# Two chained self-attention layers: stage 1's q and k masked and stacked by VectorE from PSUM, with new engine orders

## The chip, the core and the metric

The kernel runs on one core of a Trainium2 chip. The metric is the device time of one execution in microseconds (us). Engine names in rows are those of the profile: PE is TensorE's matmul, PEld its weight load, DVE VectorE, ACT ScalarE, POOL GpSimd, SP SyncE (which only issues DMAs here).

## The reference

Two self-attention layers run one after the other on x of shape (4, 128, 32, 32), that is 4 batches of 128 channels and 1024 positions. Each layer computes, for every batch:

```
q = Wq x + bq          # 16 x 1024
k = Wk x + bk          # 16 x 1024
v = Wv x + bv          # 128 x 1024
attn = softmax(q^T k)  # 1024 x 1024, over the last axis
x = gamma * (v attn^T) + x
```

All data is fp32. The second layer takes the first layer's x.

## The kernel before

**Stages.** The work is cut into eight stages s, one for each layer and batch: stages 0 to 3 are layer 0, stages 4 to 7 layer 1. Stage s + 4 needs the x that stage s finished. Inside a stage the 1024 positions are eight tiles of 128.

**What one stage does.** TensorE projects q and k together into one PSUM tile (steps `QX` and `QK`, two accumulating halves). The result is stored as fp32r, three copies of a 16-row block for each of q and k, and one of the copies is replaced by the rounding rest: a *mask* step makes a rounded copy of the masked rows, and a *stack* step subtracts that from the whole. The stacked tile `qk` is copied by two DMAs with its halves swapped (`qk_swapped`, step `swap`), and the energies are products of the two. For each tile i, TensorE makes energies (`E.s.i`), VectorE takes the negated row maximum (`max.s.i`, L563), and ScalarE takes the exponential in place and its row sum (`sum.s.i`, L472). The logarithm of the sums (`log`), split in two by GpSimd (`parts`), transposed by TensorE (`shift`), copied to SBUF by VectorE (`rows`) and placed by DMA into spare rows of `qk` (`place`), turns a second, transposed energy product (`ET.s.k`) into the logarithm of the softmax, so that one exponential (`attn`, L484) gives the finished weights. Six of eight weight tiles are cut into a high and a low part (`hi` L359, L490; `lo` L364, L558) and multiplied with a cut v (`PH`, `PV`); the other two are multiplied whole. v is projected by `VX` and `V` and evacuated by VectorE (`v32`). VectorE adds the result to x (`finish`).

**The ring.** All products but those of the weights with v go into a ring of three PSUM tiles, `ring0` to `ring2`. A step named `E.0.3.0` uses ring tile 0. Before TensorE writes a ring tile, it waits for whoever reads the tile's previous content last (`wait_for_ring`): for an energy tile that is the `sum` step, for q and k it is the evacuation.

**Stage 0 and stage 1.** Stage 0's energies are computed from plain fp32 q and k (`qk_raw`, `swapped_raw`) so that they can start early. Stage 1 is listed in `FROM_SBUF`: ScalarE copies its q and k from PSUM to the SBUF tile `unstacked` (`evac.1.0`, L466), GpSimd masks (`mask.1.0`, L407) and stacks (`stack.1.0`, L414) from there. Stages 2 to 7 have mask and stack on VectorE, both read from PSUM (L530, L537).

**Orders.** Each engine works through a list written by hand, in order: `PE_ORDER`, `ACT_ORDER`, `DVE_ORDER`, `POOL_ORDER`, `SP_ORDER`. An instruction that waits holds up everything behind it on its engine. `warm.0.n` on TensorE are n pairs of products of zeros, which write to `out_psum` and depend on nothing. `swap.1.0` stands first and `swap.0.0` second on SP's list. These lines decide who waits in the part that the diff touches:

```python
elif what == "E":
    engine.wait_ge(sum_made, nth_sum[s, i])
elif what == "QK":
    engine.wait_ge(*(evacuated, nth_evac[s, 0]) if s in FROM_SBUF else stacked(s))
```

Of the kernel before, what the change touches and what calls it, by code (L numbers as in the profile page):

```python
# [48 lines left out]


PE_ORDER = """
raw.0.0.0 raw.0.1.1 E.0.6.2 QX.1.0.0 E.0.0.1 QK.1.0.0 E.0.7.2 warm.0.2 E.0.4.0 E.0.2.1 E.0.1.2 warm.0.2 E.0.3.0
E.0.5.1 VX.0.0.2 warm.0.2 E.1.4.0 V.0.0.2 shift.0.0.1 warm.0.2 E.1.7.1 warm.0.2 QX.2.0.0 E.1.6.2 QK.2.0.0 warm.0.2
ET.0.2.1 warm.0.4 ET.0.3.2 warm.0.2 E.1.5.1 ET.0.1.0 E.1.0.2 PH.0.2 E.1.2.0 PH.0.3 shift.0.1.1 E.1.3.2 ET.0.0.1
E.1.1.0 PH.0.1 E.2.4.1 PV.0.0 E.2.7.2 ET.0.6.0 PV.0.3 VX.1.0.1 E.2.1.0 V.1.0.1 shift.1.1.2 PV.0.1 ET.0.4.2 PV.0.2
ET.0.5.0 QX.3.0.1 ET.0.7.2 E.2.3.0 QK.3.0.1 E.2.0.2 PV.0.7 ET.1.3.0 PH.0.5 ET.1.2.2 PH.0.6 E.2.6.0 ET.1.1.1 PV.0.5
E.2.2.2 PH.0.4 E.2.5.1 PV.0.6 PV.0.4 VX.2.0.0 ET.1.4.2 V.2.0.0 ET.1.6.1 PH.1.3 ET.1.5.2 PH.1.1 ET.1.7.0 ET.1.0.1
E.3.0.2 PH.1.2 shift.2.1.0 PV.1.2 E.3.1.1 QX.4.0.0 E.3.2.2 QK.4.0.0 PV.1.0 ET.2.3.1 PV.1.3 PV.1.1 ET.2.1.2 ET.2.2.0
E.3.6.1 E.3.5.2 PH.1.6 E.3.4.0 PH.1.5 PV.1.6 E.3.3.1 PH.1.4 E.3.7.2 PV.1.7 E.4.4.0 ET.2.6.1 PV.1.5 PV.1.4 VX.3.0.2
ET.2.4.1 V.3.0.2 ET.2.5.0 PH.2.3 ET.2.0.1 PH.2.1 ET.2.7.2 PV.2.3 shift.3.1.0 E.4.0.1 PH.2.2 E.4.7.0 E.4.1.2 PV.2.0  # L60
E.4.2.1 PV.2.2 PV.2.1 QX.5.0.0 ET.3.3.2 QK.5.0.0 ET.3.0.1 PH.2.6 ET.3.1.2 PH.2.4 ET.3.2.1 PV.2.6 ET.3.4.2 E.4.5.0
PH.2.5 E.4.6.1 PV.2.4 PV.2.5 ET.3.6.2 PV.2.7 ET.3.5.0 VX.4.0.2 E.4.3.1 V.4.0.2 E.5.3.0 PV.3.0 E.5.4.1 PH.3.2 E.5.6.2
shift.4.1.0 PH.3.3 E.5.2.0 PH.3.1 E.5.1.1 PV.3.3 PV.3.1 PV.3.2 QX.6.0.2 ET.4.3.0 QK.6.0.2 ET.4.2.1 PH.3.4 ET.3.7.0
E.5.7.1 PH.3.6 ET.4.1.0 PV.3.6 E.5.5.2 PH.3.5 E.5.0.0 PV.3.5 PV.3.7 E.6.6.1 ET.4.5.2 PV.3.4 VX.5.0.0 ET.4.4.2
V.5.0.0 ET.4.0.1 PH.4.3 ET.4.6.2 PV.4.3 E.6.3.0 QX.7.0.1 shift.5.1.2 PV.4.0 ET.4.7.2 E.6.2.0 QK.7.0.1 PH.4.1 PH.4.2
ET.5.1.2 PV.4.1 PV.4.2 ET.5.2.0 ET.5.3.1 ET.5.6.2 E.6.4.0 PH.4.4 E.6.0.2 PH.4.6 E.6.7.1 PH.4.5 E.6.5.0 PV.4.6 PV.4.5
E.6.1.2 PV.4.4 PV.4.7 ET.5.0.1 E.7.0.0 ET.5.5.2 E.7.4.1 PH.5.1 E.7.1.2 PV.5.0 shift.6.1.0 PH.5.3 E.7.6.1 ET.5.4.0
PV.5.1 E.7.3.2 PH.5.2 PV.5.3 PV.5.2 VX.6.0.0 E.7.2.1 ET.6.0.2 V.6.0.0 PH.5.5 ET.5.7.2 PH.5.4 ET.6.5.0 PH.5.6
ET.6.2.1 E.7.7.2 PV.5.5 PV.5.7 ET.6.4.0 ET.6.1.1 PV.5.6 PV.5.4 VX.7.0.2 E.7.5.0 ET.6.6.1 V.7.0.2 PH.6.1 PV.6.0
ET.6.7.1 ET.6.3.2 shift.7.1.0 PH.6.6 PH.6.4 PH.6.5 PH.6.3 PH.6.2 ET.7.3.0 ET.7.2.2 PV.6.2 PV.6.1 PV.6.3 PV.6.6  # L70
PV.6.5 PV.6.4 ET.7.0.1 ET.7.1.0 ET.7.6.2 PV.6.7 PH.7.2 ET.7.5.1 ET.7.4.0 ET.7.7.2 PV.7.2 PH.7.3 PV.7.0 PH.7.1 PH.7.6
PV.7.1 PV.7.3 PH.7.5 PH.7.4 PV.7.6 PV.7.5 PV.7.4 PV.7.7
"""
ACT_ORDER = """
sum.0.6 evac.1.0 sum.0.0 sum.0.7 sum.0.4 sum.0.2 sum.0.1 sum.0.3 log.0.0 sum.0.5 sum.1.4 v_hi.0.0 log.0.1 sum.1.7
sum.1.6 attn.0.2 attn.0.3 attn.0.1 sum.1.5 sum.1.0 sum.1.2 attn.0.0 sum.1.3 sum.1.1 sum.2.4 attn.0.6 log.1.1 sum.2.7
sum.2.1 attn.0.4 attn.0.5 attn.0.7 hi.0.5 sum.2.3 sum.2.0 attn.1.3 attn.1.2 attn.1.1 sum.2.6 sum.2.2 sum.2.5
attn.1.4 attn.1.6 log.2.1 attn.1.5 attn.1.7 attn.1.0 sum.3.0 hi.1.4 v_hi.2.0 sum.3.1 sum.3.2 attn.2.3 attn.2.1
attn.2.2 sum.3.6 sum.3.5 sum.3.4 sum.3.3 sum.3.7 attn.2.6 sum.4.4 log.3.1 attn.2.4 attn.2.5 attn.2.0 attn.2.7 hi.2.6
sum.4.0 sum.4.7 sum.4.1 sum.4.2 attn.3.3 attn.3.0 attn.3.1 attn.3.2 attn.3.4 sum.4.5 attn.3.6 sum.4.6 attn.3.5  # L80
hi.3.6 sum.4.3 log.4.1 sum.5.3 hi.3.5 sum.5.4 sum.5.6 sum.5.2 sum.5.1 attn.4.3 attn.4.2 attn.3.7 v_hi.4.0 attn.4.1
sum.5.7 sum.5.5 sum.5.0 attn.4.5 log.5.1 sum.6.6 attn.4.4 attn.4.0 attn.4.6 hi.4.4 sum.6.3 hi.4.6 hi.4.5 attn.4.7
sum.6.2 attn.5.1 attn.5.2 attn.5.6 attn.5.3 sum.6.4 sum.6.0 sum.6.7 sum.6.5 sum.6.1 attn.5.0 log.6.1 attn.5.5
sum.7.0 sum.7.4 sum.7.1 attn.5.4 sum.7.6 sum.7.3 attn.6.0 sum.7.2 attn.5.7 v_hi.6.0 attn.6.5 attn.6.2 sum.7.7
attn.6.4 attn.6.1 attn.6.6 sum.7.5 log.7.1 hi.6.6 hi.6.4 attn.6.3 attn.6.7 attn.7.3 v_hi.7.0 attn.7.2 hi.7.2
attn.7.0 attn.7.1 attn.7.6 attn.7.7 attn.7.5 attn.7.4 hi.7.5 hi.7.4
"""
DVE_ORDER = """
max.0.6 max.0.0 max.0.7 max.0.4 max.0.2 max.0.1 max.0.3 max.0.5 max.1.4 rows.0.0 v32.0.0 max.1.7 max.1.6 mask.2.0
stack.2.0 max.1.5 max.1.0 max.1.2 rows.0.1 max.1.3 max.1.1 max.2.4 max.2.7 max.2.1 rows.1.1 v32.1.0 finish.0.0  # L90
max.2.3 max.2.0 mask.3.0 stack.3.0 max.2.6 max.2.2 max.2.5 finish.0.1 v32.2.0 lo.1.1 max.3.0 rows.2.1 max.3.1
max.3.2 mask.4.0 stack.4.0 finish.1.0 max.3.6 max.3.5 max.3.4 max.3.3 max.3.7 max.4.4 finish.1.1 v32.3.0 lo.2.2
rows.3.1 max.4.0 max.4.7 max.4.1 max.4.2 finish.2.0 mask.5.0 stack.5.0 max.4.5 max.4.6 v_lo.3.0 finish.2.1 max.4.3
max.5.3 v32.4.0 max.5.4 rows.4.1 max.5.6 max.5.2 max.5.1 finish.3.0 mask.6.0 stack.6.0 max.5.7 max.5.5 max.5.0
max.6.6 finish.3.1 v32.5.0 max.6.3 rows.5.1 lo.4.2 max.6.2 mask.7.0 stack.7.0 finish.4.0 max.6.4 max.6.0 max.6.7
max.6.5 max.6.1 finish.4.1 max.7.0 max.7.4 max.7.1 rows.6.1 max.7.6 max.7.3 finish.5.0 max.7.2 v32.6.0 lo.5.4
max.7.7 v_lo.6.0 finish.5.1 max.7.5 v32.7.0 lo.6.5 rows.7.1 lo.6.6 lo.6.3 lo.6.4 finish.6.0 v_lo.7.0 lo.7.2
finish.6.1 lo.7.6 lo.7.5 finish.7.0 finish.7.1
"""
POOL_ORDER = """  # L100
mask.1.0 stack.1.0 parts.0.0 parts.0.1 v_lo.0.0 hi.0.2 hi.0.3 hi.0.1 lo.0.2 lo.0.3 lo.0.1 parts.1.1 hi.0.6 lo.0.6
v_hi.1.0 hi.0.4 v_lo.1.0 lo.0.5 lo.0.4 hi.1.2 hi.1.1 hi.1.3 lo.1.2 parts.2.1 lo.1.3 hi.1.6 hi.1.5 lo.1.6 lo.1.5
hi.2.1 v_lo.2.0 lo.1.4 hi.2.3 hi.2.2 lo.2.3 parts.3.1 hi.2.4 lo.2.1 v_hi.3.0 lo.2.6 hi.2.5 lo.2.4 lo.2.5 hi.3.3
hi.3.1 hi.3.2 lo.3.2 lo.3.3 parts.4.1 lo.3.1 hi.3.4 lo.3.4 lo.3.6 lo.3.5 hi.4.3 hi.4.2 v_lo.4.0 lo.4.3 hi.4.1
parts.5.1 lo.4.1 v_hi.5.0 lo.4.6 lo.4.5 hi.5.1 hi.5.2 lo.4.4 hi.5.3 v_lo.5.0 lo.5.3 parts.6.1 lo.5.1 lo.5.2 hi.5.4
hi.5.5 hi.5.6 lo.5.5 lo.5.6 hi.6.2 hi.6.1 hi.6.5 parts.7.1 lo.6.2 hi.6.3 lo.6.1 hi.7.3 lo.7.3 hi.7.1 lo.7.1 hi.7.6
lo.7.4
"""
# [724 lines left out]
```

## Time and profile before

| | us |
|---|---|
| median of 3 runs | 193.89 |
| lowest and highest run | 193.38, 194.21 |
| the profiled execution, its own time | 193.06 |
| its span, first to last instruction | 191.30 |
| busy PE, PEld | 179.1, 123.1 |
| busy DVE, ACT, POOL | 145.7, 155.5, 156.9 |

The profiled execution is 0.83 us faster than the median, and 1.76 us of its time lie outside the span. Busy times are sums over the whole span; waits and the chain of work that ended last say which of them matter at a given place. In rows of the timeline, the first number is the start in us from the span's start, the second the duration; instructions that follow each other on one line are merged, with their count behind an x.

### The profile page before, as it was taken

To read this page: it belongs to the slowest core of one execution; us is meant where nothing else is said; L and a number is where in the kernel's file an instruction comes from. 1 tells how busy PE (TensorE), PEld (TensorE's weight loads), DVE (VectorE), ACT (ScalarE), POOL (GpSimd) and SP (SyncE) were. 2 spreads that over 40 slices of the span, in tenths; PEclk is the share of its full clock that TensorE was granted. 3 is DMA by queue.
4 is the path that set the end of the run, shared out by engine and by line. 5 is a ranking of instruction groups with operands and counts; after the bars stand their busy time and mean duration, and the time that the engine had idled before them with its cause. 6 is when DMAs were issued, how large, how long until landed. Compare 5 with 4: busy or idle time off the path is not lost.

```text
...
## 1 busy us (share of the span) xinstructions
PE 179.1 (94%) x1282; PEld 123.1 (64%) x1282; DVE 145.7 (76%) x137; ACT 155.5 (81%) x223; POOL 156.9 (82%) x120
## 2 busy tenths in 40 slices
...
PEclk9999999999999999999999999999999999999999
...
GB/s 155 345 104 0 215 9 42 69 3 3 2 113 0 5 111 3 0 3 3 110 3 0 3 55 58 2 3 107 61 55 7 55 0 58 3 0 55 55 55 55
DMA packets 3890, 9.51 MB, mean 50 GB/s; under 512 B 548, under 2 KB 932, under 8 KB 3876
## 3 DMA queue, kind: packets, MB, share of 16 engines
q1 hardware_dynamic: 3876, 9.31, 16.7%
...
## 4 chain that ended last, share of the span: by engine, by line
PE 34%; POOL 31%; ACT 15%; issue 10%; DMA 4%; DVE 4%; SPq 1%; POOLq 0%; DVEq 0%; ACTq 0%
POOL attn_lo L364 14%; PE out_psum L720 10%; POOL attn_hi L359 9%; ACT ring L472 8%; PE out_psum L722 7%; ACT attn L484 4%; DMA qk_swapped<-qk 4%; PE ring L671 3%; PE ring L697 3%; PE out_psum L756 3%; PE ring L642 2%; DVE neg_max L563 2%; PE ring L624 2%; PE ring L657 2%; ACT attn_hi L490 2%
## 5 line engine op out<-in xcount | busy, mean ns | idle before, releaser
L364 POOL TENSOR_TENSOR attn_lo<-attn,attn_hi 128x1024 fp32r<-128x1024 f32 x37 | 90.4, 2455 | 1.8 <-ACT attn_hi L490 1.3
L563 DVE TENSOR_REDUCE neg_max<-ring 128x1 f32<-128x1024 f32 x64 | 75.6, 1219 | 15.7 <-PE ring L673 15.3
L472 ACT ACTIVATE ring<-ring,neg_max 128x1024 f32<-128x1024 f32 x64 | 69.6, 1087 | 9.9 <-DVE neg_max L563 9.3
L484 ACT ACTIVATE attn<-ring 128x1024 f32<-128x1024 f32 x64 | 63.3, 1024 | 9.8 <-DVE attn_lo L558 5.6
L359 POOL TENSOR_SCALAR attn_hi<-attn 128x1024 fp32r<-128x1024 f32 x35 | 39.2, 1134 | 5.5 <-ACT attn L484 5.4
L699 PE MATMUL ring<-qk_swapped,qk 64*128 64x512 f32 x64 | 29.0, 478 | 0.0
L697 PE MATMUL ring<-qk,qk_swapped 64*128 64x512 f32 x64 | 28.5, 468 | 0.3
L671 PE MATMUL ring<-qk_swapped,qk 64*128 64x512 f32 x56 | 25.1, 452 | 3.4 <-ACT attn L484 1.7
L673 PE MATMUL ring<-qk,qk_swapped 64*128 64x512 f32 x56 | 25.7, 461 | 0.0
L558 DVE TENSOR_TENSOR attn_lo<-attn,attn_hi 128x1024 fp32r<-128x1024 f32 x11 | 19.4, 1778 | 5.5 <-POOL attn_hi L359 4.7
L723 PE MATMUL out_psum<-attn_hi,v_hi 64*128 64x512 f32 x72 | 23.0, 399 | 0.0
L722 PE MATMUL out_psum<-attn_hi,v_hi 64*128 64x512 f32 x72 | 23.0, 398 | 0.0
L723 PE MATMUL out_psum<-attn,v 64*128 64x512 f32 x48 | 22.6, 590 | 0.0
L722 PE MATMUL out_psum<-attn,v 64*128 64x512 f32 x48 | 22.6, 590 | 0.0
L722 PE MATMUL out_psum<-attn_hi,v_lo 64*128 64x512 f32 x72 | 22.2, 388 | 0.0
L723 PE MATMUL out_psum<-attn_hi,v_lo 64*128 64x512 f32 x72 | 22.2, 388 | 0.0
L722 PE MATMUL out_psum<-attn_lo,v_hi 64*128 64x512 f32 x72 | 20.9, 392 | 0.1
L723 PE MATMUL out_psum<-attn_lo,v_hi 64*128 64x512 f32 x72 | 20.9, 392 | 0.0
L697 PEld LDWEIGHTS ring<-qk,qk_swapped 64*128 64x128 f32 x64 | 11.5, 184 | 10.9 <-issue 9.9
L657 PEld LDWEIGHTS ring<-late,x_all 64*128 64x128 f32 x256 | 16.6, 187 | 2.5 <-issue 1.7
L671 PEld LDWEIGHTS ring<-qk_swapped,qk 64*128 64x128 f32 x56 | 10.3, 184 | 12.3 <-issue 10.3
L657 PE MATMUL ring<-late,x_all 64*128 64x128 f32 x256 | 17.6, 275 | 0.2 <-ACT ring L472 0.2
...
## 6 DMA issues: line engine op xcount, KB each, us to landing
...
qk<-shift_rows SPq DMA_DIRECT2D x7, 8.0 KB
```

The source lines that it names most:

```text
L359: nc.gpsimd.tensor_scalar(attn_hi[:, k - 1], attn[:, k], 1.0, 0.0, ALU.mult, ALU.add).then_inc(cut_made["hi", "gpsimd"], 1)
L364: nc.gpsimd.tensor_tensor(attn_lo[:, k - 1], attn[:, k], attn_hi[:, k - 1].bitcast(fp32), ALU.subtract).then_inc(cut_made["lo", "gpsimd"], 1)
L472: nc.scalar.activation(e[:], e[:], ACT.Exp, bias=neg_max[s][:, i:i + 1], accum_out=row_sum[s][:, i:i + 1]).then_inc(sum_made, 1)
L484: nc.scalar.activation(attn[:, k], ring_tile("ET", s, k)[:].rearrange("p (a n) -> p a n", a=2), ACT.Exp).then_inc(attn_made, 1)
L563: nc.vector.tensor_reduce(neg_max[s][:, i:i + 1], ring_tile("E", s, i)[:], axis=AX.X, op=ALU.max, negate=True).then_inc(max_made, 1)
L657: last = nc.tensor.matmul(to[:, chunk], x_all[rows, s, chunk], late[rows, WV + layer(s)], start=step == 0 and j == 0, stop=step == 1 and j ...
L671: nc.tensor.matmul(to[:, 0:HALF], q_over_k[0:64, rows], k_over_q[0:64, 0:HALF], start=True, stop=True)
L673: nc.tensor.matmul(to[:, HALF:N], k_over_q[64:128, rows], q_over_k[64:128, HALF:N], start=True, stop=True).then_inc(e_mm, 1)
L697: nc.tensor.matmul(to[:, 0:HALF], k_over_q[0:64, first], q_over_k[0:64, part], start=True, stop=not added(s, h))
L699: last = nc.tensor.matmul(to[:, HALF:N], q_over_k[64:128, second], k_over_q[64:128, part], start=True, stop=not added(s, h))
L722: nc.tensor.matmul(out_psum[:, 0:HALF], v[0:64], a[0:64], start=start, stop=stop)
L723: last = nc.tensor.matmul(out_psum[:, HALF:N], v[64:128], a[64:128], start=start, stop=stop)
```

## The change

Stage 1 is taken out of `FROM_SBUF`. Its mask and stack become VectorE steps like those of stages 2 to 7, ScalarE's `evac.1.0` and GpSimd's `mask.1.0` and `stack.1.0` go, and the five orders are written anew. Compared word by word, the orders of ScalarE, VectorE, GpSimd and SP differ in these steps alone; TensorE's order keeps its sequence of steps, has the ring tiles 0 and 1 exchanged from `E.0.4` on, and other numbers of `warm` pairs up to `ET.0.3`. Every line number falls by one, because GpSimd's list is a line shorter.

```diff
-FROM_SBUF = (1,)
+FROM_SBUF = ()
...
 PE_ORDER = """
-raw.0.0.0 raw.0.1.1 E.0.6.2 QX.1.0.0 E.0.0.1 QK.1.0.0 E.0.7.2 warm.0.2 E.0.4.0 E.0.2.1 E.0.1.2 warm.0.2 E.0.3.0
-E.0.5.1 VX.0.0.2 warm.0.2 E.1.4.0 V.0.0.2 shift.0.0.1 warm.0.2 E.1.7.1 warm.0.2 QX.2.0.0 E.1.6.2 QK.2.0.0 warm.0.2
+raw.0.0.0 raw.0.1.1 warm.0.4 E.0.6.2 QX.1.0.0 E.0.0.1 QK.1.0.0 E.0.7.2 warm.0.3 E.0.4.1 warm.0.1 E.0.2.0 warm.0.5
+E.0.1.2 E.0.3.1 E.0.5.0 warm.0.1 VX.0.0.2 E.1.4.1 V.0.0.2 shift.0.0.0 warm.0.2 E.1.7.0 warm.0.2 QX.2.0.1 E.1.6.2
...
 ACT_ORDER = """
-sum.0.6 evac.1.0 sum.0.0 sum.0.7 sum.0.4 sum.0.2 sum.0.1 sum.0.3 log.0.0 sum.0.5 sum.1.4 v_hi.0.0 log.0.1 sum.1.7
+sum.0.6 sum.0.0 sum.0.7 sum.0.4 sum.0.2 sum.0.1 sum.0.3 log.0.0 sum.0.5 sum.1.4 v_hi.0.0 log.0.1 sum.1.7 sum.1.6
...
 DVE_ORDER = """
-max.0.6 max.0.0 max.0.7 max.0.4 max.0.2 max.0.1 max.0.3 max.0.5 max.1.4 rows.0.0 v32.0.0 max.1.7 max.1.6 mask.2.0
+max.0.6 max.0.0 mask.1.0 stack.1.0 max.0.7 max.0.4 max.0.2 max.0.1 max.0.3 max.0.5 max.1.4 rows.0.0 v32.0.0 max.1.7
...
 POOL_ORDER = """
-mask.1.0 stack.1.0 parts.0.0 parts.0.1 v_lo.0.0 hi.0.2 hi.0.3 hi.0.1 lo.0.2 lo.0.3 lo.0.1 parts.1.1 hi.0.6 lo.0.6
+parts.0.0 parts.0.1 v_lo.0.0 hi.0.2 hi.0.3 hi.0.1 lo.0.2 lo.0.3 lo.0.1 parts.1.1 hi.0.6 lo.0.6 v_hi.1.0 hi.0.4
```

VectorE's order around the new steps: `neg_max0` rows are `max.0.6`, `max.0.0`, `max.0.7`, `max.0.4`, `max.0.2`, `max.0.1`, `max.0.3`, `max.0.5` in this order, the `neg_max1` row is `max.1.4`. Before:

```order
L563 TENSOR_REDUCE neg_max0<-ring2 128x1 [waits e_mm]
L563 TENSOR_REDUCE neg_max0<-ring1 128x1 [waits e_mm]
L563 TENSOR_REDUCE neg_max0<-ring2 128x1 [waits e_mm]
L563 TENSOR_REDUCE neg_max0<-ring0 128x1 [waits e_mm]
L563 TENSOR_REDUCE neg_max0<-ring1 128x1 [waits e_mm]
L563 TENSOR_REDUCE neg_max0<-ring2 128x1 [waits e_mm]
L563 TENSOR_REDUCE neg_max0<-ring0 128x1 [waits e_mm]
L563 TENSOR_REDUCE neg_max0<-ring1 128x1 [waits e_mm]
L563 TENSOR_REDUCE neg_max1<-ring0 128x1 [waits e_mm]
```

And now:

```order
L562 TENSOR_REDUCE neg_max0<-ring2 128x1 [waits e_mm]
L562 TENSOR_REDUCE neg_max0<-ring1 128x1 [waits e_mm]
L529 TENSOR_SCALAR masked_hi<-ring0,weights 128x1024 [waits qk_mm]
L536 SCALAR_TENSOR_TENSOR qk1<-ring0,weights,masked_hi 128x1024 [waits masked_made]
L562 TENSOR_REDUCE neg_max0<-ring2 128x1 [waits e_mm]
L562 TENSOR_REDUCE neg_max0<-ring1 128x1 [waits e_mm]
L562 TENSOR_REDUCE neg_max0<-ring0 128x1 [waits e_mm]
L562 TENSOR_REDUCE neg_max0<-ring2 128x1 [waits e_mm]
L562 TENSOR_REDUCE neg_max0<-ring1 128x1 [waits e_mm]
L562 TENSOR_REDUCE neg_max0<-ring0 128x1 [waits e_mm]
L562 TENSOR_REDUCE neg_max1<-ring1 128x1 [waits e_mm]
```

Two instructions of 128x1024 stand between the second and the third row maximum of stage 0, with six more maxima of stage 0 behind them.

TensorE's order behind `E.0.7`: two rows of line L671 and L673 are one energy step, here `E.0.4`, `E.0.2` and `E.0.1` before:

```order
L671 MATMUL ring0<-swapped_raw,qk_raw 128x512 [waits evacuated,raw_swapped_made,raw_made]
L673 MATMUL ring0<-qk_raw,swapped_raw 128x512
L671 MATMUL ring1<-swapped_raw,qk_raw 128x512 [waits sum_made,raw_swapped_made,raw_made]
L673 MATMUL ring1<-qk_raw,swapped_raw 128x512
L671 MATMUL ring2<-swapped_raw,qk_raw 128x512 [waits sum_made,raw_swapped_made,raw_made]
L673 MATMUL ring2<-qk_raw,swapped_raw 128x512
```

And now `E.0.4`, a warm pair and `E.0.2`:

```order
L670 MATMUL ring1<-swapped_raw,qk_raw 128x512 [waits sum_made,raw_swapped_made,raw_made]
L672 MATMUL ring1<-qk_raw,swapped_raw 128x512
L755 MATMUL out_psum<-zeros 128x512
L756 MATMUL out_psum<-zeros 128x512
L670 MATMUL ring0<-swapped_raw,qk_raw 128x512 [waits qk_made,raw_swapped_made,raw_made]
L672 MATMUL ring0<-qk_raw,swapped_raw 128x512
```

The ring tile that held stage 1's q and k went to `E.0.4` after ScalarE's copy; it now goes to `E.0.2` after VectorE's stack.

TensorE's order around stage 1's first energies, `E.1.4`. Before, from `VX.0.0` on:

```order
L657 MATMUL ring2<-late,x_all 128x128 [waits x0_loaded1,sum_made,x0_loaded0,late_loaded]
L657 MATMUL ring2<-late,x_all 128x128 x7
L756 MATMUL out_psum<-zeros 128x512
L757 MATMUL out_psum<-zeros 128x512
L756 MATMUL out_psum<-zeros 128x512
L757 MATMUL out_psum<-zeros 128x512
L671 MATMUL ring0<-qk_swapped1,qk1 128x512 [waits sum_made,swapped1]
L673 MATMUL ring0<-qk1,qk_swapped1 128x512
```

And now:

```order
L755 MATMUL out_psum<-zeros 128x512
L756 MATMUL out_psum<-zeros 128x512
L656 MATMUL ring2<-late,x_all 128x128 [waits x0_loaded1,sum_made,x0_loaded0,late_loaded]
L656 MATMUL ring2<-late,x_all 128x128 x7
L670 MATMUL ring1<-qk_swapped1,qk1 128x512 [waits sum_made,swapped1]
L672 MATMUL ring1<-qk1,qk_swapped1 128x512
```

In both orders `E.1.4` waits for the swapped copy of stage 1's q and k and for the sum that frees its ring tile, which is `sum.0.3` in both.

## Rows read from the trace of the kernel before

**Rows 1.** The page: busy time, and PE's granted clock in 40 slices.

```profile
PE 179.1 (94%) x1282; PEld 123.1 (64%) x1282; DVE 145.7 (76%) x137; ACT 155.5 (81%) x223; POOL 156.9 (82%) x120
...
PEclk9999999999999999999999999999999999999999
```

**Rows 2.** The chain that ended last, 8 to 34 us: start us, us, what.

```profile
13.76 1.12 ACT unstacked L466
...
14.97 1.13 POOL masked_hi L407
...
16.17 2.35 POOL qk L414
18.54 0.56 SPq L323
...
19.15 3.82 DMA qk_swapped<-qk
...
23.02 0.49 PE ring L671
```

**Rows 3.** Timeline of ScalarE: `sum.0.7`, `sum.0.1`, `sum.0.3`, `sum.1.4`.

```profile
16.22 1.09 ACT L472 ACTIVATE ring<-ring,neg_max 128x1024 f32<-128x1024 f32 x1 [0.25 <-DVE neg_max L563]
...
20.00 1.09 ACT L472 ACTIVATE ring<-ring,neg_max 128x1024 f32<-128x1024 f32 x1
...
21.29 1.09 ACT L472 ACTIVATE ring<-ring,neg_max 128x1024 f32<-128x1024 f32 x1
...
24.81 1.09 ACT L472 ACTIVATE ring<-ring,neg_max 128x1024 f32<-128x1024 f32 x1 [0.99 <-DVE neg_max L563]
```

**Rows 4.** Timeline of TensorE: `E.0.6`, `E.0.1`, `E.0.3`, `VX.0.0`, two warm pairs (first product).

```profile
10.02 0.66 PE L671 MATMUL ring<-swapped_raw,qk_raw 64*128 64x512 f32 x1 [0.94 <-DVE swapped_raw L519]
...
17.57 0.66 PE L671 MATMUL ring<-swapped_raw,qk_raw 64*128 64x512 f32 x1 [0.33 <-ACT ring L472]
...
18.93 0.59 PE L671 MATMUL ring<-swapped_raw,qk_raw 64*128 64x512 f32 x1
...
21.34 1.16 PE L657 MATMUL ring<-late,x_all 64*128 64x128 f32 x16 [0.23 <-ACT ring L472]
22.31 0.38 PE L756 MATMUL out_psum<-zeros 64*128 64x512 bf16 x1
...
22.53 0.38 PE L756 MATMUL out_psum<-zeros 64*128 64x512 bf16 x1
```

**Rows 5.** Timeline of VectorE: `max.0.0`; the six maxima behind it; `max.1.4`.

```profile
12.90 1.22 DVE L563 TENSOR_REDUCE neg_max<-ring 128x1 f32<-128x1024 f32 x1 [0.49 <-PE ring L673]
14.96 7.42 DVE L563 TENSOR_REDUCE neg_max<-ring 128x1 f32<-128x1024 f32 x6 [0.83 <-PE ring L673]
23.55 1.22 DVE L563 TENSOR_REDUCE neg_max<-ring 128x1 f32<-128x1024 f32 x1 [1.17 <-PE ring L673]
```

**Rows 6.** Timeline of VectorE, narrower windows: `max.0.1`; `max.0.3`, each with its follower.

```profile
18.74 2.51 DVE L563 TENSOR_REDUCE neg_max<-ring 128x1 f32<-128x1024 f32 x2
...
20.02 2.36 DVE L563 TENSOR_REDUCE neg_max<-ring 128x1 f32<-128x1024 f32 x2
```

**Rows 7.** Timeline of VectorE at stage 2's mask and stack, and of SP behind them.

```profile
27.56 1.22 DVE L563 TENSOR_REDUCE neg_max<-ring 128x1 f32<-128x1024 f32 x1 [0.34 <-PE ring L673]
28.70 1.33 DVE L530 TENSOR_SCALAR masked_hi<-ring,weights 128x1024 fp32r<-128x1024 f32 x1
30.07 1.28 DVE L537 SCALAR_TENSOR_TENSOR qk<-ring,weights,masked_hi 128x1024 fp32r<-128x1024 f32 x1
...
31.38 0.53 SPq L323 DMA_DIRECT2D qk_swapped<-qk  x1
```

**Rows 8.** Timeline of GpSimd: ahead of stage 1's mask; behind its stack, the first `parts`.

```profile
12.14 0.72 POOL L431 TENSOR_SCALAR units<-units 128x640 fp32r<-128x640 f32 x1
...
22.87 0.20 POOL L391 TENSOR_TENSOR shift<-neg_max,log_sum 128x4 f32<-128x4 f32 x1 [4.36 <-ACT log_sum L479]
```

**Rows 9.** Busy time by stretch: us, engines, granted clock, DMA share, GB/s.

```profile
14.12:23.50 9.38, 8.75 (x58) 3.81 (x56) 7.17 (x7) 8.78 (x15) 3.92 (x5) 1.00 0.40 100
```

More of the change, by code:

```diff
@@ L51 @@
 PE_ORDER = """
-raw.0.0.0 raw.0.1.1 E.0.6.2 QX.1.0.0 E.0.0.1 QK.1.0.0 E.0.7.2 warm.0.2 E.0.4.0 E.0.2.1 E.0.1.2 warm.0.2 E.0.3.0
-E.0.5.1 VX.0.0.2 warm.0.2 E.1.4.0 V.0.0.2 shift.0.0.1 warm.0.2 E.1.7.1 warm.0.2 QX.2.0.0 E.1.6.2 QK.2.0.0 warm.0.2
-ET.0.2.1 warm.0.4 ET.0.3.2 warm.0.2 E.1.5.1 ET.0.1.0 E.1.0.2 PH.0.2 E.1.2.0 PH.0.3 shift.0.1.1 E.1.3.2 ET.0.0.1
-E.1.1.0 PH.0.1 E.2.4.1 PV.0.0 E.2.7.2 ET.0.6.0 PV.0.3 VX.1.0.1 E.2.1.0 V.1.0.1 shift.1.1.2 PV.0.1 ET.0.4.2 PV.0.2
-ET.0.5.0 QX.3.0.1 ET.0.7.2 E.2.3.0 QK.3.0.1 E.2.0.2 PV.0.7 ET.1.3.0 PH.0.5 ET.1.2.2 PH.0.6 E.2.6.0 ET.1.1.1 PV.0.5
@@ L57 @@
[L57 to L71, printed above, removed]
@@ L72 @@
-PV.7.1 PV.7.3 PH.7.5 PH.7.4 PV.7.6 PV.7.5 PV.7.4 PV.7.7
+raw.0.0.0 raw.0.1.1 warm.0.4 E.0.6.2 QX.1.0.0 E.0.0.1 QK.1.0.0 E.0.7.2 warm.0.3 E.0.4.1 warm.0.1 E.0.2.0 warm.0.5
+E.0.1.2 E.0.3.1 E.0.5.0 warm.0.1 VX.0.0.2 E.1.4.1 V.0.0.2 shift.0.0.0 warm.0.2 E.1.7.0 warm.0.2 QX.2.0.1 E.1.6.2
+QK.2.0.1 warm.0.2 ET.0.2.0 warm.0.3 ET.0.3.2 warm.0.2 E.1.5.0 ET.0.1.1 E.1.0.2 PH.0.2 E.1.2.1 PH.0.3 shift.0.1.0
+E.1.3.2 ET.0.0.0 E.1.1.1 PH.0.1 E.2.4.0 PV.0.0 E.2.7.2 ET.0.6.1 PV.0.3 VX.1.0.0 E.2.1.1 V.1.0.0 shift.1.1.2 PV.0.1
@@ new lines @@
+ET.0.4.2 PV.0.2 ET.0.5.1 QX.3.0.0 ET.0.7.2 E.2.3.1 QK.3.0.0 E.2.0.2 PV.0.7 ET.1.3.1 PH.0.5 ET.1.2.2 PH.0.6 E.2.6.1
+ET.1.1.0 PV.0.5 E.2.2.2 PH.0.4 E.2.5.0 PV.0.6 PV.0.4 VX.2.0.1 ET.1.4.2 V.2.0.1 ET.1.6.0 PH.1.3 ET.1.5.2 PH.1.1
+ET.1.7.1 ET.1.0.0 E.3.0.2 PH.1.2 shift.2.1.1 PV.1.2 E.3.1.0 QX.4.0.1 E.3.2.2 QK.4.0.1 PV.1.0 ET.2.3.0 PV.1.3 PV.1.1
+ET.2.1.2 ET.2.2.1 E.3.6.0 E.3.5.2 PH.1.6 E.3.4.1 PH.1.5 PV.1.6 E.3.3.0 PH.1.4 E.3.7.2 PV.1.7 E.4.4.1 ET.2.6.0 PV.1.5
+PV.1.4 VX.3.0.2 ET.2.4.0 V.3.0.2 ET.2.5.1 PH.2.3 ET.2.0.0 PH.2.1 ET.2.7.2 PV.2.3 shift.3.1.1 E.4.0.0 PH.2.2 E.4.7.1
@@ new lines @@
+E.4.1.2 PV.2.0 E.4.2.0 PV.2.2 PV.2.1 QX.5.0.1 ET.3.3.2 QK.5.0.1 ET.3.0.0 PH.2.6 ET.3.1.2 PH.2.4 ET.3.2.0 PV.2.6
+ET.3.4.2 E.4.5.1 PH.2.5 E.4.6.0 PV.2.4 PV.2.5 ET.3.6.2 PV.2.7 ET.3.5.1 VX.4.0.2 E.4.3.0 V.4.0.2 E.5.3.1 PV.3.0
+E.5.4.0 PH.3.2 E.5.6.2 shift.4.1.1 PH.3.3 E.5.2.1 PH.3.1 E.5.1.0 PV.3.3 PV.3.1 PV.3.2 QX.6.0.2 ET.4.3.1 QK.6.0.2
+ET.4.2.0 PH.3.4 ET.3.7.1 E.5.7.0 PH.3.6 ET.4.1.1 PV.3.6 E.5.5.2 PH.3.5 E.5.0.1 PV.3.5 PV.3.7 E.6.6.0 ET.4.5.2 PV.3.4
+VX.5.0.1 ET.4.4.2 V.5.0.1 ET.4.0.0 PH.4.3 ET.4.6.2 PV.4.3 E.6.3.1 QX.7.0.0 shift.5.1.2 PV.4.0 ET.4.7.2 E.6.2.1
```

56 lines of the change are left out of this document (31 added, 25 removed).

## The prediction

> **What bounds the kernel now.** I read the page's busy times first, then the chain that ended last, then the timelines of the engines between 8 and 34 us, where the edit lies. The busy times name no single bound: PE shows 94%, GpSimd 82%, ScalarE 81%, VectorE 76% [rows 1], and they are averages over stages with different limits. The chain is what counts at one place, and it runs straight through the edited steps: ScalarE's copy at 13.76, GpSimd's mask at 14.97 and stack at 16.17, the swap DMA at 18.54, its landing, and stage 1's first energies E.1.4 at 23.02 [rows 2]. So the removed work is on the path. But a chain shows only what ended last. E.1.4 waits for two things: the swapped copy, and the ring tile that sum.0.3 frees. From the start of a sum to the product that takes its tile, the timelines show 1.35 us (sum.0.7 at 16.22 [rows 3], E.0.1 at 17.57 [rows 4]). sum.0.3 begins at 21.29 [rows 3], so the tile was free for a product at 21.29 + 1.35 = 22.64. **The second wait ends only 0.38 us ahead of the first.** However early the swap lands, E.1.4 can win no more than 0.38 us unless stage 0's sums also come earlier, and these hang on VectorE's maxima, to which the change adds two instructions.
>
> **What goes.** ScalarE loses 1.12 us, GpSimd 1.13 + 2.35 = 3.48 us [rows 2]. GpSimd's next instruction comes at 22.87 after 4.36 us of waiting for a logarithm [rows 8]: its relief lengthens a wait and gives nothing directly. ScalarE waits for VectorE's maxima on both sides of this part (0.25 and 0.99 us in [rows 3]), so its relief gives nothing unless the maxima come earlier.
>
> **When q and k are ready.** Stage 2 has the same pair of instructions on VectorE, with a row maximum ahead: maximum 27.56, mask 28.70, stack 30.07, swap DMA 31.38 [rows 7], that is 1.14, 1.37 and 1.31 us apart. Stage 1's pair now stands behind max.0.0, which starts at 12.90 [rows 5]; its q and k are there at 13.76, when ScalarE's copy could start. Mask at 12.90 + 1.14 = 14.04, stack at 15.41, end of the stack at 15.41 + 1.28 = 16.69, swap DMA at 16.72. That is 18.54 - 16.72 = 1.82 us earlier than now. From the issue to E.1.4 now pass 23.02 - 18.54 = 4.48 us [rows 2], so the swapped copy lands by about 21.20. On SP swap.0.0 stands behind swap.1.0 and moves with it; no new wait arises there.
>
> **What VectorE's queue pays.** The third maximum, max.0.7, now starts at 14.96 after 0.83 us of idleness [rows 5]. Behind the stack it starts at 16.69: 1.73 us later. The pair costs 2.65 us and the idle time hides the rest. Then three engines take turns around three ring tiles, and I follow the tiles with the distances that the timelines show:
>
> - max.0.7 at 16.69; sum.0.7 1.26 later (14.96 to 16.22), 17.95; E.0.1 1.35 later, 19.30; max.0.1 1.17 later (17.57 to 18.74 [rows 4, 6]), 20.47.
> - max.0.4 follows max.0.7 by 1.14, the closest that two neighbours come (two from 20.02 on take 2.36 [rows 6], less 1.22 for the second): 17.83. sum.0.4 1.26 later, 19.09; E.0.3 1.35 later, 20.44; max.0.3 1.09 later (18.93 to 20.02), 21.53, but VectorE is free 1.14 after max.0.1, at 21.61.
> - sum.0.3 follows max.0.3 by 1.27 (20.02 to 21.29): 22.88. **E.1.4 follows 1.35 later, at 24.23**, against 23.02 now: 1.21 us late.
>
> Two other things come before E.1.4 on TensorE and end earlier. The swap has landed by 21.20. VX.0.0 waits for sum.0.1: 20.47 + 1.26 = 21.73, VX 1.34 later (20.00 to 21.34), 23.07, and TensorE takes its next step 0.97 later (21.34 to 22.31 [rows 4]), at 24.04. E.0.2 now waits for the stack, until 16.69, in place of sum.0.0; behind it stand five warm pairs and E.0.1, which cannot start before 19.30 anyway.
>
> **Warm pairs.** Four pairs now stand ahead of E.0.6. TensorE idles 0.94 us there [rows 4]. Pairs follow each other by 0.22 us behind VX.0.0 (22.31 to 22.53), and one product takes 0.38 by itself [rows 4]. From 9.08, where that idle time begins, four pairs end at 9.96 in the first case and at 10.60 if nothing overlaps. I take the first value, since those are pairs among other products as these are: no cost, against an upper end of 10.60 - 10.02 = 0.58. The granted clock is 1.00, the 2.4 GHz level, in this stretch [rows 9] and everywhere [rows 1], also around that idle time of 0.94 us; the new waits on TensorE that I find are shorter (E.1.4 waits 24.23 - 24.04 = 0.19). I charge nothing for the clock.
>
> **Where the delay goes.** Behind E.1.4 the steps of every engine stand as before, and all engines depend on it: max.1.4 starts 0.53 later (now 23.55 [rows 5]), sum.1.4 follows max.1.4 (24.81 [rows 3]), and each later stage follows from these. ScalarE and GpSimd reach this point 1.2 to 1.7 us late too, since sum.0.3 and the logarithm behind it move by 22.88 - 21.29 = 1.59. No queue arrives less late than 1.21, and nothing that is done by then (the loads) sets a time later. A queue system in which everything starts 1.2 us late ends 1.2 us late. So the profiled execution would go from 193.06 to 193.06 + 1.21 = 194.27 us. The profiled execution lies 0.83 under the median of the runs, so I put the same sum on the median: 193.89 + 1.21 = **195.1 us**, 0.6% slower.
>
> Unknown here are two prices. VectorE's step from a stack to a maximum is not shown without a wait; it lies between 1.14, as from a maximum on, and the 1.37 from mask to stack, where the second waits for the first [rows 7]; I take 1.28, the stack's own length. And the later sums may run at VectorE's closest distance (1.14 each), or keep all of the 1.73: max.0.3 then starts four steps after 16.69, at 21.25, and E.1.4 at 23.87 (0.85 late), or E.1.4 is 1.73 late. This gives the forecast's own bounds, 0.85 to 1.73 late, less 0.14 or plus 0.09 for the first price.
>
> **Rivals.**
>
> 1. *The delay is given back* (no difference to measure). If the maxima run 1.14 apart, E.1.4 is 0.85 late, 194.7; if a later stage swallows the delay, 193.9. For it: VectorE idles 1.17 us before max.1.4 [rows 5], and later stages contain many small waits. Against it: that idle time lies behind the maxima that are late, and the ring needs 1.26 + 1.35 + 1.17 = 3.78 us for a round of three tiles, more than three times 1.14. Chance 0.2.
> 2. *The earlier swap wins* (not slower). VectorE's pair would have to fit wholly into its idle time, and E.1.4 would start when the tile is free, at 22.64: 193.89 - 0.38 = 193.5. It decides at 2.65 us of idleness ahead of the maxima; the trace shows 0.83. Chance 0.06.
> 3. *GpSimd's total load is the bound.* It is the busiest engine but PE [rows 1], and the 3.48 us taken from it could come off the end: 190.4. Against it speak the 4.36 us it waits right behind the removed work [rows 8]. The Trainium skill ("Perfetto Trace Analysis", Identifying the Most-Contended Engine) says to take the engine of highest occupancy as the bottleneck and to leave out matmul busy time; by this rule this rival is the one to expect. The trace of this stretch disagrees: GpSimd is busy 3.92 of 9.38 us there [rows 9]. Chance 0.04.
> 4. *Worse.* The pair's 1.73 us reach the end in full, and E.0.6 starts late behind the warm pairs, 0.58 at most: up to 193.89 + 1.73 + 0.58 = 196.2, at half of that price for the warm pairs 195.9. Chance 0.1.
>
> **How the numbers follow.** The forecast keeps 0.6. Its middle, 1.21 us, is close to what a measurement of this kernel can tell from no change, about 0.5% or 0.97 us; the runs themselves spread from 193.38 to 194.21. I count 0.1 of the forecast's 0.6 as within 0.5%. Faster by more than 0.5%: rival 3, 0.04, and 0.01 for the spread. Within: 0.2 + 0.06 + 0.1 - 0.01 = 0.35. Slower: 0.5 + 0.1 = 0.6. The range goes from 193.9, the end of rival 1, to 196.1, which takes in the forecast's upper bound (193.89 + 1.82 = 195.7) and most of rival 4; rivals 2 and 3 and the tails are left out.
>
> **What would show it.** In the profile of the changed kernel: mask at about 14.0 and the stack's end at 16.7 on VectorE; the swap DMA near 16.7; max.0.7 right behind the stack with no idle time; E.1.4 near 24.2, released by ScalarE's sum and no longer by the DMA; max.1.4 near 24.75; GpSimd waiting from 12.86, the end of its last step ahead of the removed ones [rows 8], to about 24.5 for the first logarithm; the span about 1.2 us longer. I am wrong if E.1.4 starts before 23.0, or if it starts late and the end does not move.

## The result and the profile after

| | before | changed |
|---|---|---|
| median, us (20 runs each) | 193.53 | 194.74 |
| lowest and highest, us | 192.57, 194.21 | 193.77, 195.38 |
| profiled execution: own time, span, us | 193.06, 191.30 | 194.92, 193.10 |

The ratio of changed to before is 1.0062, with a 95% interval of 1.0046 to 1.0078: 0.62% slower, 1.20 us on 193.53 (0.89 to 1.51). 195.1 was predicted on a median of 193.89, that is 1.21 us more.

First the page of the changed kernel, busy time and granted clock. They answer to [rows 1]:

```profile
PE 182.3 (94%) x1296; PEld 123.5 (64%) x1296; DVE 148.6 (77%) x139; ACT 154.5 (80%) x222; POOL 153.6 (80%) x118
...
PEclk9999999999999999999999999999999999999999
```

GpSimd lost 3.3 us of work, ScalarE 1.0, VectorE gained 2.9, and the kernel became slower. No busy time tells that; the timelines of the first 26 us do. VectorE, from max.0.0 to max.1.4 (answers to [rows 5, 7]):

```profile
13.81 1.23 DVE L562 TENSOR_REDUCE neg_max<-ring 128x1 f32<-128x1024 f32 x1 [0.49 <-PE ring L672]
14.95 1.34 DVE L529 TENSOR_SCALAR masked_hi<-ring,weights 128x1024 fp32r<-128x1024 f32 x1
16.32 1.28 DVE L536 SCALAR_TENSOR_TENSOR qk<-ring,weights,masked_hi 128x1024 fp32r<-128x1024 f32 x1
17.53 3.48 DVE L562 TENSOR_REDUCE neg_max<-ring 128x1 f32<-128x1024 f32 x3
21.29 3.49 DVE L562 TENSOR_REDUCE neg_max<-ring 128x1 f32<-128x1024 f32 x3 [0.29 <-PE ring L672]
25.57 1.23 DVE L562 TENSOR_REDUCE neg_max<-ring 128x1 f32<-128x1024 f32 x1 [0.79 <-PE ring L672]
```

ScalarE's sum.0.7 and sum.0.3, and TensorE's E.0.1, VX.0.0 and E.1.4, all from timelines (answer to [rows 3, 4]):

```profile
18.78 1.09 ACT L471 ACTIVATE ring<-ring,neg_max 128x1024 f32<-128x1024 f32 x1 [2.50 <-DVE neg_max L562]
...
23.68 1.09 ACT L471 ACTIVATE ring<-ring,neg_max 128x1024 f32<-128x1024 f32 x1
```

```profile
20.13 0.66 PE L670 MATMUL ring<-swapped_raw,qk_raw 64*128 64x512 f32 x1 [0.16 <-ACT ring L471]
...
23.90 1.16 PE L656 MATMUL ring<-late,x_all 64*128 64x128 f32 x16 [0.17 <-ACT ring L471]
25.03 0.46 PE L670 MATMUL ring<-qk_swapped,qk 64*128 64x512 f32 x1
```

SP's first swap DMA, and GpSimd's first `parts` instruction (answers to [rows 8]):

```profile
17.64 0.56 SPq L322 DMA_DIRECT2D qk_swapped<-qk  x1
```

```profile
25.28 0.20 POOL L390 TENSOR_TENSOR shift<-neg_max,log_sum 128x4 f32<-128x4 f32 x1 [11.50 <-ACT log_sum L478]
```

This execution as a whole began later: max.0.0 starts at 13.81 instead of 12.90 [rows 5], because its first projections ended 0.9 us later. That is no work of the change; the last section shows it in rows. So everything below is counted from the start of max.0.0. From there, the swap DMA starts at 3.83 (before: 5.64) and E.1.4 at 11.22 (before: 10.12). **The swap started 1.8 us earlier and the energies that it feeds 1.10 us later.** Where ScalarE waited 0.25 us for max.0.7 [rows 3], it now waits 2.50.

### The profile page after: what moved, and what is told of

It reads as the page before. It is cut to its first block, busy times and chain, and to the rows that moved or that the text cites. A ratio compares the mean times of both kernels' runs of the same rounds, so it can differ in the third digit from the quotient of the medians.

```text
span 193.1 us, 3509 instructions
## 1 busy us (share of the span) xinstructions
PE 182.3 (94%) x1296; PEld 123.5 (64%) x1296; DVE 148.6 (77%) x139; ACT 154.5 (80%) x222; POOL 153.6 (80%) x118
## 4 chain that ended last, share of the span: by engine, by line
PE 39%; POOL 28%; ACT 15%; issue 10%; DVE 6%; POOLq 0%; ACTq 0%; DVEq 0%
POOL attn_lo L363 14%; PE out_psum L719 10%; PE out_psum L721 10%; POOL attn_hi L358 9%; ACT ring L471 9%; ACT attn L483 4%; PE ring L670 4%; DVE neg_max L562 4%; PE ring L696 3%; PE out_psum L755 3%; PE ring L656 2%; PE ring L623 2%; PE ring L641 2%; ACT attn_hi L489 2%; POOL shift L390 1%
```

## Experiments

Each was compared with the kernel before in five rounds on one chip; the chip is not the same for all of them. The table has, for one profiled execution of each, two distances from the start of max.0.0: to E.1.4, and to VectorE's last instruction of the program. Between them stands the distance from the start of sum.0.3, which frees the ring tile of E.1.4, to E.1.4.

| kernel | E.1.4 | from sum.0.3 to E.1.4 | last step | ratio to before (95% interval) |
|---|---|---|---|---|
| before | 10.12 | 1.73 | 175.17 | |
| changed | 11.22 | 1.35 | 176.10 | 1.0062 (1.0046 to 1.0078) |
| one spare maximum | 10.08 | 1.50 | 175.23 | 1.0002 (0.9974 to 1.0031) |
| three spare maxima | 14.40 | 1.34 | 179.80 | 1.0214 (1.0177 to 1.0251) |
| changed, old TensorE order | 11.49 | 1.35 | 176.63 | 1.0087 (1.0059 to 1.0115) |
| changed, max.0.7 between | 11.79 | 1.35 | 176.69 | 1.0084 (1.0055 to 1.0113) |
| the same, five warm pairs less | 11.09 | 1.35 | 176.22 | 1.0051 (1.0027 to 1.0076) |
| three spare maxima, ten warm pairs more | 12.19 | 1.35 | 177.41 | 1.0114 (1.0079 to 1.0149) |
| before, swap.0.0 first | 9.91 | 1.52 | 175.07 | 0.9984 (0.9959 to 1.0009) |
| the same, two warm pairs less | 9.91 | 1.52 | 174.84 | 1.0001 (0.9980 to 1.0022) |

In all nine kernels the last step moves with E.1.4, within 0.35 us, over a stretch of 165 us. So E.1.4 is a good marker of what a kernel loses here; the sums and logarithms beside it move too, and no run delays E.1.4 alone.

In the six kernels that lost time E.1.4 starts 1.34 to 1.35 us after sum.0.3, the distance from a sum to the product that takes its tile. In the other four it starts later than that. The loss comes through the tile.

### One spare maximum on VectorE

```diff
-max.0.6 max.0.0 max.0.7 ...
+max.0.6 max.0.0 spare.0.0 max.0.7 ...
...
+                nc.vector.tensor_reduce(spare[n][:], swapped_raw[:], axis=AX.X, op=ALU.max,
+                                        negate=True).then_inc(spare_made, 1)
```

> The kernel before, with one more row maximum on VectorE, of an SBUF tile and used by nobody, between max.0.0 and max.0.7; nothing else changes. Theory (the maxima hand VectorE's delay around the ring): one costs about 1.14 us from max.0.0 on, so max.0.7 starts 12.90 + 2 x 1.14 = 15.18 instead of 14.96 on the clock of the trace before, 0.2 late; E.1.4 keeps its time, 10.1 us after the start of max.0.0, because the swap's landing ends 0.38 later than its ring tile. Time: same as before within 0.2 us. Rival (VectorE's load as such): every microsecond given to VectorE costs, 0.7 to 1.2 us slower.

Timeline of VectorE (L545 is the spare maximum):

```profile
13.59 1.23 DVE L570 TENSOR_REDUCE neg_max<-ring 128x1 f32<-128x1024 f32 x1 [0.49 <-PE ring L682]
14.73 1.21 DVE L545 TENSOR_REDUCE spare<-swapped_raw 128x1 f32<-128x1024 f32 x1
15.85 3.48 DVE L570 TENSOR_REDUCE neg_max<-ring 128x1 f32<-128x1024 f32 x3
```

max.0.7 starts 2.26 after max.0.0, 0.20 later than before, as expected; E.1.4 came at 10.08, and the time is the same. The work of 1.21 us filled the idle time of 0.83 us in [rows 5], and the 0.20 by which max.0.7 came late stayed below the 0.38 by which the ring tile is free ahead of the swap's landing. VectorE's load as such costs nothing here: the 0.7 us of that rival lie above the interval's upper end, 0.6 us.

### Three spare maxima

The same edit with three.

> As the run with one spare maximum, but three. Theory: max.0.7 starts at 12.90 + 4 x 1.14 = 17.46, 2.5 late; E.1.4 follows 7.5 us later, at about 25.0 on the clock of the trace before, that is 12.0 to 12.1 us after the start of max.0.0 (before: 10.12); 1.9 to 2.0 us slower than before. ScalarE's copy and GpSimd's mask and stack are still there, so a loss of this size needs neither their removal nor the new TensorE order. Rival (new order of TensorE is what costs): no loss here. Rival (VectorE's load as such): three times the run with one, 2.1 to 3.4 us.

A loss of 2.1%, about 4.1 us, twice what was expected, in a kernel that has neither the removals nor the new TensorE order. The maxima did what was worked out: max.0.7 starts 4.52 after max.0.0, for 4.56.

```profile
13.49 1.23 DVE L570 TENSOR_REDUCE neg_max<-ring 128x1 f32<-128x1024 f32 x1 [0.49 <-PE ring L682]
14.63 3.46 DVE L545 TENSOR_REDUCE spare<-swapped_raw 128x1 f32<-128x1024 f32 x3
18.01 3.48 DVE L570 TENSOR_REDUCE neg_max<-ring 128x1 f32<-128x1024 f32 x3
```

The rest happened on TensorE. Its timeline at E.0.1 and E.1.4, and the busy time by stretch (us, then PE, PEld, DVE, ACT, POOL, granted clock, DMA share, GB/s):

```profile
20.61 1.19 PE L680 MATMUL ring<-swapped_raw,qk_raw 64*128 64x512 f32 x1 [2.78 <-ACT ring L474]
...
27.89 0.57 PE L680 MATMUL ring<-qk_swapped,qk 64*128 64x512 f32 x1
```

```profile
17.00:20.60 3.60, 0.83 (x4) 0.02 (x2) 3.60 (x4) 1.34 (x3) 2.11 (x1) 0.91 0.08 19
20.60:26.00 5.40, 5.39 (x16) 2.48 (x18) 2.83 (x3) 3.33 (x6) 0.00 (x0) 0.50 0.74 181
26.00:32.00 6.00, 5.82 (x60) 3.65 (x56) 5.20 (x6) 4.62 (x9) 0.61 (x3) 0.94 0.01 3
```

TensorE idled 2.78 us ahead of E.0.1. The granted clock fell during this wait: it is 0.50, the level of 1.2 GHz, from 20.00 on, and 1.00 again from 27.00 on. The first product of E.0.1 takes 1.19 us where it took 0.66 [rows 4]. That this was the rest of the loss is tested further below, with ten warm pairs.

### The changed kernel with the old TensorE order

```diff
-... QK.1.0.0 E.0.7.2 warm.0.3 E.0.4.1 warm.0.1 E.0.2.0 warm.0.5 E.0.1.2 ...
+... QK.1.0.0 E.0.7.2 warm.0.2 E.0.4.0 E.0.2.1 E.0.1.2 warm.0.2 ...
```

> The changed kernel, but with TensorE's order of before, word for word: the old ring tiles (E.0.4 takes the tile of stage 1's q and k and waits for VectorE's stack, E.0.2 waits for sum.0.0) and the old warm pairs. Theory: E.0.4 is out before VectorE is back from the stack or at most 0.15 us after, so E.1.4 stays 11.2 to 11.4 us after the start of max.0.0 and the time is that of the changed kernel, 1.2 us (1.0 to 1.4) over the kernel before. Rival (ring tiles or warm pairs of the new order cost): it falls back to the kernel before, less than 0.4 us over it.

Timeline of TensorE: E.0.4 and E.1.4.

```profile
16.90 0.66 PE L670 MATMUL ring<-swapped_raw,qk_raw 64*128 64x512 f32 x1 [1.49 <-DVE qk L536]
...
24.45 0.47 PE L670 MATMUL ring<-qk_swapped,qk 64*128 64x512 f32 x1
```

E.0.4 now waits 1.49 us for the stack, and VectorE waits 0.18 for E.0.4. E.1.4 comes at 11.49, 0.09 past the expected range, and the time is 1.7 us (1.1 to 2.2) over the kernel before, for 1.0 to 1.4. The loss is all there, so it doesn't come from the new ring tiles or warm pairs; in the profile these are worth 0.27 us to the changed kernel, in the runs they can't be told apart. The granted clock stayed 1.00 over those 1.49 us.

### max.0.7 between mask and stack

```diff
-max.0.6 max.0.0 mask.1.0 stack.1.0 max.0.7 max.0.4
+max.0.6 max.0.0 mask.1.0 max.0.7 stack.1.0 max.0.4
```

> The changed kernel, with max.0.7 moved between mask and stack on VectorE. Theory: max.0.7 starts about 1.2 us earlier against max.0.0 (2.5 instead of 3.7), so its ring tile turns earlier, while max.0.4 stays where it is; from there the maxima run 1.14 apart; the swap starts 1.2 us later and still lands in time (about 9.4 us after the start of max.0.0). E.1.4 comes 10.9 to 11.0 us after the start of max.0.0 instead of 11.2: 0.2 to 0.4 us faster than the changed kernel, 0.8 to 1.0 us slower than the kernel before. Rival (the swap's landing decides): 1.2 us slower than the changed kernel.

A miss: E.1.4 comes at 11.79 where 10.9 to 11.0 was expected, later than in the changed kernel and not earlier. The time is 1.6 us over the kernel before (1.1 to 2.2) where 0.8 to 1.0 was expected; against the changed kernel it can't be told apart. Timeline of ScalarE at sum.0.7, then of TensorE: E.0.2, the first product of E.0.1, E.1.4.

```profile
17.37 1.09 ACT L471 ACTIVATE ring<-ring,neg_max 128x1024 f32<-128x1024 f32 x1 [1.18 <-DVE neg_max L562]
```

```profile
18.68 0.66 PE L670 MATMUL ring<-swapped_raw,qk_raw 64*128 64x512 f32 x1 [0.99 <-DVE qk L536]
...
20.69 0.59 PE L670 MATMUL ring<-swapped_raw,qk_raw 64*128 64x512 f32 x1
...
25.52 0.49 PE L670 MATMUL ring<-qk_swapped,qk 64*128 64x512 f32 x1
```

max.0.7 moved ahead as planned, and sum.0.7 began at 17.37, so E.0.1's tile was free at 17.37 + 1.35 = 18.72. But E.0.1 stands behind E.0.2 and five warm pairs on TensorE, and E.0.2 waited for the stack, which was now later: E.0.1 came at 20.69. The expectation followed the tiles and forgot the queue. The swap started 4.83 after max.0.0, 1.0 later than in the changed kernel, and no row shows a wait for it.

### The same without the five warm pairs

```diff
-E.0.2.0 warm.0.5 E.0.1.2
+E.0.2.0 E.0.1.2
```

> The run with max.0.7 between mask and stack, without the five warm pairs behind E.0.2. That run missed its time; reading of the miss: E.0.2 waits for the later stack, and E.0.1 stands behind it and behind five warm pairs on TensorE, though its own tile is free 0.6 us or more before. Then, without the pairs, E.0.1 starts 5.8 us after the start of max.0.0 instead of 7.0, max.0.1 at 7.25, max.0.3 at 8.5, E.1.4 at 11.0 to 11.1 (with the pairs: 11.79; changed kernel: 11.22): 0.6 to 0.8 us faster than with the pairs, 0.9 to 1.1 over the kernel before. Rival (the swap, which starts 1.0 later than in the changed kernel, decides): no gain from taking the pairs out.

Timeline of TensorE: the first product of E.0.1, and E.1.4.

```profile
18.55 0.59 PE L670 MATMUL ring<-swapped_raw,qk_raw 64*128 64x512 f32 x1
...
23.76 0.47 PE L670 MATMUL ring<-qk_swapped,qk 64*128 64x512 f32 x1
```

max.0.0 starts at 12.67 here: E.0.1 comes 5.88 after it for the expected 5.8, E.1.4 at 11.09 for 11.0 to 11.1. The time is 0.51% over the kernel before, 1.0 us, as expected. The queue was the reason of the miss. This placement of the pair gets back about 0.1 us of the 1.1 in the profile. Other placements, say the stack behind more of the maxima, weren't tried.

### Three spare maxima with ten warm pairs

The run with three spare maxima, with one change on TensorE's list:

```diff
-E.0.2.1 E.0.1.2
+E.0.2.1 warm.0.10 E.0.1.2
```

> The run with three spare maxima, with ten warm pairs added in front of E.0.1, where TensorE idled 2.78 us and then ran at its lower level. Theory: the granted clock stays 1.00, E.1.4 comes 12.0 to 12.1 us after the start of max.0.0 (without the pairs 14.4), and the time is 1.9 to 2.1 us over the kernel before: VectorE's delay as it was worked out, and the rest of that run's 4.1 us was the clock. Rival (three maxima delay more than worked out): still 3 to 4 us over the kernel before.

Timeline of TensorE: E.0.1 and E.1.4.

```profile
20.76 0.66 PE L680 MATMUL ring<-swapped_raw,qk_raw 64*128 64x512 f32 x1 [0.62 <-ACT ring L474]
...
25.83 0.50 PE L680 MATMUL ring<-qk_swapped,qk 64*128 64x512 f32 x1
```

The line of the wait says 0.62 us instead of 2.78, the granted clock is 1.00 throughout, and E.1.4 comes at 12.19 instead of 14.40, while E.0.1 starts 7.12 after max.0.0 in both. So 2.21 us of the run without warm pairs were the clock, and VectorE's delay alone costs 2.07 at E.1.4 (1.9 to 2.0 was worked out) and 1.14% of the time, 2.2 us (1.5 to 2.9).

### swap.0.0 ahead of swap.1.0

The kernel before, with one change on SP's list:

```diff
-swap.1.0 swap.0.0 place.0.0
+swap.0.0 swap.1.0 place.0.0
```

> The kernel before, with swap.0.0 ahead of swap.1.0 on SP's list: stage 0's swap, ready about 6 us earlier, is out of the way when stage 1's starts. Theory: the swap lands earlier (3.7 us or less instead of 4.5 from issue to E.1.4), and E.1.4 wins what its ring tile leaves, 0.38 us, and no more: 9.7 to 9.8 us after the start of max.0.0 instead of 10.12; time 0.3 to 0.4 us under the kernel before. Rival (only the swap decides): E.1.4 wins all that the swap wins, 0.7 us or more. Rival (the two swaps do not disturb each other): no gain.

The chain that ended last no longer holds ScalarE's copy, GpSimd's work or the swap. It goes through the maxima, the sums and TensorE:

```profile
20.30 0.02 issue
20.32 1.22 ACT ring L472 x2
21.53 0.14 issue
21.67 1.16 PE ring L657 x16
22.83 0.18 PE out_psum L756
...
23.26 0.37 PE ring L671
```

E.1.4 won 0.21 us, at 9.91 where 9.7 to 9.8 was expected, and the chain now names VX.0.0 and two warm pairs right in front of it. But from the swap's issue (18.86) to E.1.4 (23.13) still pass 4.27 us, 0.21 less than before, where 3.7 or less was expected. The swap itself may set E.1.4 here as well. The ratio of 0.9984 can't be told from 1.

### The same without these two warm pairs

The run with swap.0.0 first, with one change on TensorE's list:

```diff
-VX.0.0.2 warm.0.2 E.1.4.0
+VX.0.0.2 E.1.4.0
```

> The kernel before, with swap.0.0 ahead of swap.1.0 and without the two warm pairs between VX.0.0 and E.1.4. In the run with swap.0.0 first, E.1.4 came 9.91 us after the start of max.0.0, behind VX.0.0 and these two pairs on TensorE. Theory: with the pairs gone the next bound is the ring tile, sum.0.3 plus 1.35: 9.74, unless the swap lands later than that (its second half starts 6.15 after max.0.0 and takes about 3.4, so 9.55). E.1.4 at 9.7 to 9.8; time 0.3 to 0.4 us under the kernel before, which lies at the edge of what five rounds can tell. Rival (nothing more to win): 9.9 as before, 0.1 to 0.2 us.

```profile
22.59 0.50 PE L671 MATMUL ring<-qk_swapped,qk 64*128 64x512 f32 x1 [0.31 <-DMA qk_swapped<-qk]
```

A miss: E.1.4 stays at 9.91, released by the swap's landing, again 4.27 us after its issue (18.32). So the two pairs were not what kept E.1.4 from starting earlier, and an early swap.0.0 shortened the swap by 0.21 us only. Neither run took the swap out of E.1.4's way. Neither kernel is shown to beat the one before.

## Why the prediction was right

- **"However early the swap lands, E.1.4 can win no more than 0.38 us."** Right, and the ground of the sign. In the changed kernel sum.0.3 starts 1.48 us later after max.0.0 than before, with three spare maxima and ten warm pairs 2.45, and E.1.4 1.10 and 2.07: 0.38 less in both. What an earlier swap alone would win wasn't measured, since in the two runs made for it the swap itself still came last or level with the rest, at a gain of 0.21. The reading of the kernel before left out a third bound: the two warm pairs behind VX.0.0 hold TensorE until about 22.75 (22.53 + 0.22 [rows 4], an estimate), so that the win would have been nearer to 0.27.
- **q and k ready.** The swap DMA was put 3.82 after max.0.0 (16.72 - 12.90); it came at 3.83.
- **VectorE's queue.** max.0.7 was put 3.79 after max.0.0 and came at 3.72: from stack to maximum pass 1.21, where 1.28 was taken and 1.14 and 1.37 were the bounds. E.0.1 came at 6.32 for 6.40, E.1.4 at 11.22 for 11.33. The experiments bear the mechanism out from both sides of the change's own 1.66 us of delay at max.0.7: 0.20 us cost nothing, 2.46 cost 2.1 at E.1.4.
- **What releases E.1.4.** sum.0.3 starts at 23.68, and 23.68 + 1.35 = 25.03 is the start of E.1.4. The chain of this profile names VX.0.0 instead, which stands in front on TensorE and whose modelled end is 25.06. The two can't be told apart in this trace, but they can across traces: the distance from sum.0.3 stays at 1.34 to 1.35 in all six kernels that lost time, while that from VX.0.0 goes from 1.13 to 1.41 among those at full clock. The tile released E.1.4, as predicted; the swap did not.
- **Warm pairs and clock at no cost.** E.0.6 starts 0.90 us after VectorE's `swapped_raw`, for which it waits, in both traces (9.12 to 10.02, 10.03 to 10.93), so the four pairs in front of it cost nothing, and the granted clock is 1.00 around it. Rows of VectorE, before (its E.0.6 is in [rows 4]) and changed, and of TensorE, changed:

```profile
9.12 0.75 DVE L519 TENSOR_SCALAR swapped_raw<-ring,weights 128x512 f32<-128x512 f32 x1 [0.89 <-PE ring L624]
```

```profile
10.03 0.75 DVE L518 TENSOR_SCALAR swapped_raw<-ring,weights 128x512 f32<-128x512 f32 x1 [0.89 <-PE ring L623]
```

```profile
10.93 0.66 PE L670 MATMUL ring<-swapped_raw,qk_raw 64*128 64x512 f32 x1
```

  Charging nothing was right for the waits that the change makes and is no rule: 2.78 us of idleness cost 2.21 us in the run with three spare maxima. The Trainium skill ("TensorE: Matmul & The Clock Gate", What's actually happening) says that the lower clock is the default and activity lifts it; the stretches of that run agree: 0.50 in the stretch behind the wait, and 0.94 in the next one, with TensorE at work all through the first of the two.
- **The delay reaches the end.** 1.10 us at E.1.4 are 0.93 at VectorE's last step. A part is given back at a later stage's swap: from VectorE's stack to the energies behind it pass 5.85 us before and 5.63 after. Chain of the kernel before, then of the changed one:

```profile
111.00 1.30 DVE qk L537
...
116.85 0.50 PE ring L671
```

```profile
118.67 0.50 PE ring L670
```

  The changed kernel's stack starts at 113.04. Before, the energies waited 0.24 us for the DMA; after, TensorE's products in front ended last. Rival 1 was right to that extent, 0.2 us in this trace.
- **GpSimd as the bound** (rival 3). The Trainium skill ("Perfetto Trace Analysis", Identifying the Most-Contended Engine) would have the engine of highest occupancy be the bottleneck. GpSimd was relieved of 3.3 us and waited 11.50 us in one piece instead of 2.10 ahead of the removed work and 4.36 behind it [rows 8]; none of the 3.3 us came off the end. This speaks against the rule where the work stands in a gap, though no run relieves GpSimd without loading VectorE. GpSimd before, at the mask:

```profile
14.97 1.12 POOL L407 TENSOR_SCALAR masked_hi<-unstacked,weights 128x1024 fp32r<-128x1024 f32 x1 [2.10 <-ACT unstacked L466]
```

The profiled execution was put at 194.27 and took 194.92. The 0.65 between are, to 0.02, the later start of that execution (0.91) less what the delay fell short of (1.21 less 0.93). That the medians differ by 1.21 us exactly as predicted is luck in part: the trace shows 0.93 to 1.10, and the interval goes from 0.89 to 1.51.
